# Macaron transformer block (FFN mixture, attention, MoE, FFN mixture): stage barriers without GpSimd's drain, a later wait for the front's last stores, and the mixture's bias adds in pairs

## The reference, cut to what matters

```
x = x + 0.5 * ffn(layernorm(x))          # f1: 16 experts + a shared part
x = x + attention_and_moe(layernorm(x))  # m: linear attention, then 8 experts
x = x + 0.5 * ffn(layernorm(x))          # f2: the same weights as f1

# ffn: every expert takes its 512 best tokens (T = 4096, F = 1024, D = 256)
topk_score, topk_ids = top_k(sigmoid(h @ gate_w.T).T, 512)
eo  = silu(xin @ gw + gb) * (xin @ up_w + up_b)
eo  = (eo @ down_w + down_b) * topk_score
out = zeros.at[topk_ids].add(eo) + shared(h)

# moe: 8 experts of capacity 1280, two experts per token
h   = gelu(x[tok] @ W1[e] + b1[e]) @ W2[e] + b2[e]
out = out.at[tok].add(gate * h)
```

## Time and profile before

| what | value |
|---|---|
| device time, median of 3 (range) | 2471.45 us (2471.08 to 2472.17) |
| device time of the profiled execution | 2471.66 us |
| its span, first to last instruction | 2469.9 us |
| TensorE busy | 92% of the span |
| VectorE busy | 67% |
| ScalarE busy | 36% |
| GpSimd busy | 35% |
| mean granted TensorE clock | 0.943 |

### The profile page before, as it was taken

The page is one execution under the profiler, slowest core; times in us unless marked ns, Lnnn a source line. Parts: engine busy times, 40 slices in busy tenths (PEclk is TensorE's granted clock), DMA queues, the critical chain, the costliest instruction groups (busy, mean ns, idle before and its releaser), DMA issues. The chain is left out here.

```text
span 2469.9 us, 37981 instructions
## 1 busy us (share of the span) xinstructions
PE 2270.3 (92%) x13564; PEld 1972.7 (80%) x13564; DVE 1662.2 (67%) x3588; ACT 891.9 (36%) x1623; POOL 876.2 (35%) x902
## 2 busy tenths in 40 slices
PE   6998999999996899963899999995998999999997
PEld 5887888888885677761799999984887888888887
DVE  5775777777774666655566666654685777777775
ACT  5222333333332666510233333335221333333332
POOL 4201323333322677620244444444211223323232
PEclk9998999999998899955899999997997999999999
DMA  5003445444443100031244444435103445445442
GB/s 174 26 28 118 112 134 133 130 129 110 139 127 83 57 18 20 20 97 38 81 81 82 83 81 80 81 42 175 29 27 104 119 120 134 116 129 136 127 130 44
DMA packets 153848, 228.21 MB, mean 92 GB/s; under 512 B 32960, under 2 KB 104384, under 8 KB 153536
## 3 DMA queue, kind: packets, MB, share of 16 engines
q1 hardware_dynamic: 102832, 157.82, 20.2%
q0 software_dynamic: 39936, 55.93, 13.4%
q10 hardware_dynamic: 10896, 12.07, 1.4%
HBM read 171.36 MB, written 54.39 MB: 91 GB/s over the span
## 5 line engine op out<-in xcount | busy, mean ns | idle before, releaser
L1082 ACT ACTIVATE me_act_f<-me_in,me_bias 128x512 f32<-128x512 f32 (+1 forms) x192 | 119.1, 620 | 294.5 <-PE me_in L125 293.6
L1082 ACT ACTIVATE f1e_silu<-f1e_in,f1e_bias 128x512 f32<-128x512 f32 (+1 forms) x136 | 90.1, 663 | 341.1 <-PE f1e_in L125 293.0
L1082 ACT ACTIVATE f2e_silu<-f2e_in,f2e_bias 128x512 f32<-128x512 f32 (+1 forms) x136 | 90.1, 663 | 341.1 <-PE f2e_in L125 292.8
L123 PE MATMUL f2e_in<-f2e_xt_hi,f2e_w_hi 128*128 128x512 f32 (+1 forms) x544 | 208.7, 384 | 3.8 <-DVE f2e_xt_lo L1143 2.3
L123 PE MATMUL f1e_in<-f1e_xt_hi,f1e_w_hi 128*128 128x512 f32 (+1 forms) x544 | 208.5, 383 | 3.9 <-DVE f1e_xt_lo L1143 2.3
L125 PE MATMUL f2e_in<-f2e_xt_hi,f2e_w_lo 128*128 128x512 f32 (+1 forms) x544 | 207.9, 382 | 0.0
L125 PE MATMUL f1e_in<-f1e_xt_hi,f1e_w_lo 128*128 128x512 f32 (+1 forms) x544 | 207.9, 382 | 0.0
L124 PE MATMUL f2e_in<-f2e_xt_lo,f2e_w_hi 128*128 128x512 f32 (+1 forms) x544 | 207.4, 381 | 0.0
L124 PE MATMUL f1e_in<-f1e_xt_lo,f1e_w_hi 128*128 128x512 f32 (+1 forms) x544 | 207.4, 381 | 0.0
L123 PE MATMUL me_down<-me_w_hi,me_act_hi 128*128 128x256 f32 x640 | 182.8, 286 | 0.0
L124 PE MATMUL me_down<-me_w_lo,me_act_hi 128*128 128x256 f32 x640 | 179.7, 281 | 0.0
(11 more groups left out here) (447 smaller groups left out, 6988.8 us busy)
## 6 DMA issues: line engine op xcount, KB each, us to landing
f_raw<-in_ffn_w SPq DMA_DIRECT2D x256, 384.0 KB, 3.6
m_raw<-in_moe_w SPq DMA_DIRECT2D x64, 256.0 KB, 2.8
f1s_x_all<-in_x SPq DMA_DIRECT2D x8, 512.0 KB, 8.8
after_ffn<-f1s_out SPq DMA_DIRECT2D x8, 512.0 KB, 2.9
after_moe<-ma_x_all SPq DMA_DIRECT2D x32, 128.0 KB, 1.7
m_h<-mr_h SPq DMA_DIRECT2D x16, 256.0 KB, 2.2
f2s_x_all<-after_moe SPq DMA_DIRECT2D x8, 512.0 KB, 8.1
out<-f2s_out SPq DMA_DIRECT2D x8, 512.0 KB, 2.9
```

What stands on the lines that cost most here:

```text
L123: pe.matmul(out, lh, rh, start=first, stop=False, skip_group_check=True)
L1082: act.activation(dst[:, st % 2, 0:n], ps_in[st % 2][0][:, 0:n], func, bias=bias[:, b, f:f + 1]).then_inc(silu_done, 1)
```

## The change

Four edits. Every `Block` is made with `no_gpsimd_drain=True`: GpSimd's DRAIN ahead of the first barrier of a stage end is gone; on the other engines the DRAIN, which also reported before, becomes a DRAIN and a separate report. `Scope.clear` is as before, with its DRAINs. The semaphores of the accumulator's stores now belong to the outer scope (`First.stored`), so that they outlive the front. SyncE ends the front with a wait for the first three of each buffer's four stores; GpSimd waits for the fourth in the experts' stage, at the head of its work on expert 0, which is ahead of its first scatter. In the mixture, experts 0 to 6 have their bias adds in pairs of tiles instead of whole chunks, one pair behind each of five steps; the last expert and the FFN stages keep theirs.

```diff
 class First:
+        self.stored = [scope.sem(f"stored{u}") for u in range(2)]
     def for_experts(self):
-        return self.ident, self.raw, self.rows, self.raw_in, self.rows_in
+        return self.ident, self.raw, self.rows, self.raw_in, self.rows_in, self.stored
...
-        out_stored = [s.sem(f"out_stored{u}") for u in range(2)]
+        out_stored = first.stored
...
-        block = s.enter_context(nc.Block())
+        block = s.enter_context(nc.Block(no_gpsimd_drain=True))
...
             sp.wait_ge(shown_out, 16)
             for u in range(2):
-                sp.wait_ge(out_stored[u], 16 * (G // 2))
+                sp.wait_ge(out_stored[u], 16 * (G // 2 - 1))
...
+        def in_chunks(e):
+
+            return gated or e == E - 1
...
             def one(e, b, left):
 
+                if gated and e == 0:
+                    for u in range(2):
+                        pool.wait_ge(acc_stored[u], 16 * (T // GT // 2))
                 if left > 1:
                     rows_free(e + 1)
...
-            def add_bias(e, st, b):
+            def add_bias(e, b, c, tiles):
 
-                c = at_step(e, st)[1]
                 dve.wait_ge(gates_set, e + 1)
                 dve.wait_ge(read_out, e * C + (c + 1 + READ0))
-                for j in range(*chunks(e)[c]):
+                for j in tiles:
                     dve.scalar_tensor_tensor(out[:, b, j, :], db[:, b], gcol[:, b, j:j + 1], out[:, b, j, :],
                                              ALU.mult, ALU.add).then_inc(out_done, 1)
 
+            def add_chunk(e, st, b):
+                if ends_at(e, st) and in_chunks(e):
+                    c = at_step(e, st)[1]
+                    add_bias(e, b, c, range(*chunks(e)[c]))
+
+            def add_pair(e, p):
+                if not in_chunks(e):
+                    add_bias(e, e % 2, 2 * p // 4, range(2 * p, 2 * p + 2))
...
                 for st in range(LAG, steps(e)):
                     activate(e, st, b)
-                    if ends_at(e, st - LAG):
-                        add_bias(e, st - LAG, b)
+                    add_chunk(e, st - LAG, b)
+                    if st == steps(e) - 1:
+                        add_pair(e, 0)
+                    if e and LAG <= st < NI - 1:
+                        add_pair(e - 1, st + 1)
...
                 for st in range(LAG):
                     if left:
                         activate(e + 1, st, 1 - b)
                         next_slice(e + 1, st, left - 1)
-                    if ends_at(e, steps(e) - LAG + st):
-                        add_bias(e, steps(e) - LAG + st, b)
+                    add_chunk(e, steps(e) - LAG + st, b)
+                    add_pair(e, st + 1)
```

More of the change, by code:

```diff
@@ L879, in run_experts @@
     AHEAD = 4
-    ident, raw, rows, raw_in, rows_in = first
+    ident, raw, rows, raw_in, rows_in, acc_stored = first
     LAG = 2
```

## The result

The changed kernel takes 2449.88 us (median of 4 runs, 2447.99 to 2450.31), the kernel before 2471.81 (median of 4, 2471.08 to 2476.25). The ratio is 0.9906, with an interval of 0.9889 to 0.9923: 21.9 us or 0.9% less time, where 2464.4 was forecast and 2459.0 to 2469.9 given as range. The time lies 9 us under the range, at rival C.

What follows compares the result with a forecast made beforehand. TensorE was taken to bound the kernel nearly everywhere, leaving only idle time to shorten. Pairs 5.5 + fronts 1.1 + lists 0.25 + expert ends 0.45 - reports 0.2 = 7.1 us off 2471.45 gave 2464.4, range 2459.0 to 2469.9.

Steps and rivals of the forecast that it cites:

- rival C: Line 77's DRAIN stays at 0.1 us everywhere, as the removed one did something of its own: about 2449 us, 8%.
- What then comes due is the DRAIN of line 77.: Stage ends: GpSimd's kept DRAIN behind the first barrier takes over the removed one's work, 2.0 us in each front.
- The expert ends: Ends of the three expert stages: line 77 takes the DRAIN over, leaving 0.15 us gained each, 0.45 in all.
- a DRAIN here has a price of its own of at least 2 us behind DMA work of GpSimd: Stage ends: GpSimd's DRAIN costs 2 us or more even when it starts long after the DMA work.
- the 2.0 that I took: Front ends: length assumed for line 77's DRAIN, from the front's own DRAIN ending 2.0 us after the last gather.
- The fronts: Ends of both fronts: 2.4 us from the moved stores' wait, plus 0.15, less 2.0: 0.55 each, 1.1 us gained.
- The lists: End of the lists stage: line 77 takes over about 2.0 us, leaving 0.25 us gained, bounds 0 and 3.4.
- The pairs: Mixture's expert boundaries: two bias adds instead of four before the split, 6 x 0.79 + 0.77 = 5.5 us gained.
- The cover for the deferred adds: Mixture: VectorE's idle time and GpSimd's waits, about 20 us per expert, hide the deferred adds and later scatters: no cost.
- The separate reports: Eight barriers: the other engines' DRAINs now have a separate report, costing 0.2 us in all, bounds 0 and 0.5.
- The stores' wait on GpSimd and the loads behind the last store: After the fronts: wait some 30 us ahead of its scatter, bias and weight loads issued up to 2.4 us earlier: no cost.
- A's range: Main case, all the forecast's terms together, 55%: 2461.5 to 2467.5 us, from bounds of pairs, fronts and separate reports.

Runs made afterwards that it cites:

- the better order of the pairs: Every deferred pair of bias adds one step later in the mixture, against the changed kernel: 2445.47 us, ratio 0.9882 to the kernel before.

## Why the prediction was wrong

**The step that failed** is "What then comes due is the DRAIN of line 77. [...] I expect the work to move into it." It doesn't move. From the earlier trace rows I took the shortness of line 77's DRAIN for the shortness of any DRAIN behind another; the two aren't the same instruction. Line 77's carries a range of semaphores to reset, and the runs show that this kind doesn't pay the plain one's price for GpSimd's indirect DMAs (0.08 us where the plain one, put into the same place, took 2.58). What the plain one does in that time no row shows. Against rival C the text held that "the two are the same instruction of the same engine": this was read from the name in the rows, which is the same for both.

**Point by point.**
- The expert ends, forecast 3 x 0.15 us: 2.65 and 3.05 in the FFNs' windows, and the mixture's end was 3.97 of its 10.25. These are the removed DRAINs of 2.58, 2.58 and 3.97 us, whole, 9.1 us in place of 0.45. A flag alone gave 12.9 us.
- "a DRAIN here has a price of its own of at least 2 us behind DMA work of GpSimd" was half right: it is a price and no wait, but of 0.082 us for each indirect DMA, as long as they are few. For the 4 gathers of a front it is 0.4 us, so even a plain DRAIN there would not have cost the 2.0 that I took.
- The fronts, forecast 1.1 us for both: 1.35 + 2.8 = 4.15. The 2.4 us each were sized rightly (the kernel with this edit alone gives them in the first front), and the 2.0 that were taken off did not come. In the first front TensorE, and with it VectorE and SyncE, was 1.0 us late by the granted clock, and SyncE's DRAIN stands at 213.9 in place of the forecast 212.9.
- The lists, forecast 0.25: 2.5. GpSimd's DRAIN waited there for the last gather to land (2.7 to 3.1 us from issue to landing for all of this line). The L77 DRAIN waits only for the gather instruction to end: the last one started at 1161.47 and took 0.95 us, to 1162.42, and the DRAIN of 1262 ns ended at 1162.50. The next stage waits for the rows by its own semaphore and could begin meanwhile.
- The pairs, forecast 5.5: 4.8 in the gaps, 5.3 in the window of the stage. The gap is 0.67 and not 0.54, since w_lo ahead of the pair waits for ScalarE (1.20 us of idle time now), so that the pair begins 1.42 us before the end of the old expert's last product (1245.42 to 1246.84), where the burst of four began 1.55 us before it (1253.84 to 1255.39, which is 1256.72 less its gap). The forecast of 0.79 us for each boundary is close to the 0.77 by which an expert as a whole got shorter. The cover for the deferred adds held: TensorE's waits show no split that is late behind them.
- The separate reports, +0.2: VectorE's begins about 0.05 us behind the end of its DRAIN (213.28 to 213.33). That is a few hundredths for a barrier, and no run tells it from nothing.
- The stores' wait on GpSimd and the loads behind the last store cost nothing: no row of the changed profile shows GpSimd waiting for the stores, and TensorE's first product comes 4.2 us after the first transpose as before (215.57 to 219.77, before 216.96 to 221.16).
- Rival C named what happened and gave 2449; it had a chance of 8%. It was ruled nearly out by an argument, and not by a row.
- A slip in the sums that changes nothing: with the bounds that it names, and the other terms as they stand, A's range comes out at 2461.9 to 2467.9, and the text has 2461.5 to 2467.5.

Open: 0.8 us of the router and 0.3 of attention, which no edit explains. The mixture has some 1 us beyond the pairs' and the DRAIN, and it lies at its start: up to the first boundary it took 84.71 us in place of 86.32, of which 0.66 are the gap, and the granted clock of that stretch was 0.88 in place of 0.86. The kernel with the bias adds alone has 85.21 us there. TensorE's granted clock averaged 0.99 in place of 0.98 in both FFN expert stages, which may be part of their 0.1 to 0.5 us beyond the DRAIN. The kernel with the better order of the pairs, too, gains more than its gaps: 5.0 us in the window for 4.0 of them.

## What to carry to other kernels

Before pricing an instruction that is removed by the row of its neighbour with the same name, look at what the two carry: here a plain DRAIN and one that resets semaphores differ by 2.5 us behind the same work. A plain GpSimd DRAIN behind indirect DMAs is a cost of its own, which here grew with their number up to 68 and was 2.6 to 5.1 us beyond; where the stage's own semaphores already prove that they landed, it can go, and it was worth its full length where GpSimd was last at a barrier. And when work is spread out to shorten a burst on the path, look at what still stands ahead of the critical split: one step later cost nothing here and took the rest of the gap. Last, before a stage of a single profile is read to the microsecond, its granted clock is to be compared: here it hid 1 us of a gain of 2.4.

## What the runs showed of the hardware

- A plain GpSimd DRAIN: 0.04 us plus 0.082 us for each indirect DMA (128 rows) since the last DRAIN, exact to 0.02 us from 8 to 68 of them; 88, 100, 124, 136 and 156 cost 4.2, 5.1, 2.6, 4.5 and 4.0. It also waits for gathers in flight (3.20 us with four gathers just issued, 0.40 when they had landed).
- The DRAIN with a range to reset took 0.065 to 0.141 us behind the same DMAs (1.26 where a gather instruction was still running), and a plain DRAIN behind it 0.040 to 0.051; the count for the next plain DRAIN starts anew behind them.
- In both fronts the granted clock fell for a few us, some 50 us into the stage, for longer in some executions than in others (0.83 or 0.66 over 10 us in the first; 0.66, 0.83 or 1.00 in the second), worth 1 us in the first and up to 3 us in the second.
